# Ten tiles of the shared FFN computed in pieces among the experts of a sparse layer, added to the output in two groups

## The reference

```
scores = softmax(xf @ gate_w.T)                     # 64 experts
topk_w, topk_idx = top_k(scores, 6)
buf_tok[e], buf_w[e] = the rows of expert e and their weights   # 128 slots an expert
gx = xf[buf_tok]                                    # gather, (64, 128, 512)
g, u = split(gx @ gate_up_proj)                     # 64 x (512, 384)
eo = (silu(g) * u) @ down_proj * buf_w              # 64 x (192, 512)
routed = zeros.at[buf_tok].add(eo)                  # scatter with addition
shared = (silu(xf @ shared_gate.T) * (xf @ shared_up.T)) @ shared_down.T   # inner size 384
x = x + routed + shared
```

## Time and profile before

| | |
|---|---|
| median of three runs | 1262.53 us |
| the profiled execution | 1266.02 us |
| its span, first to last instruction | 1263.9 us |
| TensorE busy | 1150.1 us (91%) |
| VectorE, ScalarE, GpSimd busy | 829.8, 548.4, 697.2 us |
| DMA | 204.89 MB, mean 162 GB/s |
| first instruction of `c_up` / last one's start | 857.0 / 1241.0 us |

### The profile page before, as it was taken

The page is one execution under the profiler, slowest core; times in us unless marked ns, Lnnn a source line. Parts: engine busy times, 40 slices in busy tenths (PEclk is TensorE's granted clock), DMA queues, the critical chain, the costliest instruction groups (busy, mean ns, idle before and its releaser), DMA issues.

```text
span 1263.9 us, 17889 instructions
## 1 busy us (share of the span) xinstructions
PE 1150.1 (91%) x5241; PEld 877.6 (69%) x5241; DVE 829.8 (66%) x1369; ACT 548.4 (43%) x1012; POOL 697.2 (55%) x404
## 2 busy tenths in 40 slices
PE   2999999999999999999879999999888989888884
PEld 1777777777777777777768889986555656555552
DVE  1677787778777777877679994645555555545543
ACT  5455555555556555654412222214334443334331
POOL 4988988888898889887030000012433544444342
PEclk8999999999999999999889999999999899889987
DMA  6224423432343244332376344456999999999995
GB/s 198 75 74 121 118 81 102 120 102 81 118 120 100 81 120 120 90 100 69 123 169 198 101 124 121 114 156 179 304 287 287 260 308 293 271 287 277 305 244 86
DMA packets 93402, 204.89 MB, mean 162 GB/s; under 512 B 15495, under 2 KB 24455, under 8 KB 93232
## 3 DMA queue, kind: packets, MB, share of 16 engines
q1 hardware_dynamic: 78256, 168.23, 45.0%
q0 software_dynamic: 15104, 36.16, 12.5%
HBM read 152.65 MB, written 52.22 MB: 162 GB/s over the span
## 4 chain that ended last, share of the span: by engine, by line
PE 57%; DMA 19%; issue 8%; DVE 8%; ACT 4%; POOL 2%; SPq 1%; POOLq 0%; DVEq 0%; ACTq 0%
PE Y L546 10%; PE Y L421 8%; PE Y L423 7%; PE Y L422 7%; DMA out_dram<-o,idx_b 6%; DMA out_dram<-w,idx_b 5%; PE Y L630 4%; DMA stage<-xn_rows,idx_i 4%; PE Y L425 3%; PE OT L564 3%; PE DX L564 3%; PE DX L404 2%; ACT xn L758 2%; PE DX L444 2%; DVE s L1147 2%
## 5 line engine op out<-in xcount | busy, mean ns | idle before, releaser
L970 POOL TENSOR_TENSOR ring<-vT,cT 128x1024 f32<-128x1024 f32 x128 | 249.2, 1957 | 73.5 <-ACT vT L738 38.7
L421 PE MATMUL Y<-split,toep 128*128 128x512 f32 x576 | 250.4, 435 | 10.2 <-POOL split L978 10.2
L1102 DVE TENSOR_TENSOR z<-Y,cT 128x1024 f32<-128x1024 f32 x128 | 156.1, 1220 | 125.1 <-PE Y L425 89.4
L978 POOL TENSOR_TENSOR split<-ring,split 128x1024 fp32r<-128x1024 f32 x96 | 230.0, 2396 | 0.0
L423 PE MATMUL Y<-split,toep 128*128 128x512 f32 x576 | 228.5, 397 | 0.0
L422 PE MATMUL Y<-split,toep 128*128 128x512 f32 x576 | 228.3, 396 | 0.0
L630 PE MATMUL Y<-ring,xT 128*128 128x384 f32 x512 | 203.4, 523 | 14.6 <-DMA ring<-in_L_ffn_down_proj_dram 14.6
L1014 POOL DMA_INDIRECT stage<-xn_rows,idx_i x64 | 68.8, 1075 | 222.7 <-issue 207.4
L546 PE MATMUL Y<-split 128*128 128x384 f32 x768 | 152.0, 347 | 4.2 <-DVE split L1161 4.2
L1107 DVE TENSOR_REDUCE o<-z 128x128 f32<-128x1024 f32 x128 | 154.4, 1206 | 1.1
L546 PEld LDWEIGHTS Y<-split 128*128 128x128 f32 x768 | 137.9, 194 | 7.5 <-DVE split L1161 3.0
(11 more groups left out here) (150 smaller groups left out, 1872.9 us busy)
## 6 DMA issues: line engine op xcount, KB each, us to landing
ring<-_L_ffn_gate_up_proj_dram SPq DMA_DIRECT2D x64, 768.0 KB
ring<-in_L_ffn_down_proj_dram SPq DMA_DIRECT2D x64, 384.0 KB
gr<-filters SPq DMA_DIRECT2D x32, 512.0 KB, 3.8
stage<-in_x_dram SPq DMA_DIRECT2D x32, 256.0 KB, 3.5
stage<-in_ctx_dram SPq DMA_DIRECT2D x32, 256.0 KB, 3.7
x_rows<-stage SPq DMA_DIRECT2D x32, 256.0 KB, 3.2
xn_rows<-xn SPq DMA_DIRECT2D x32, 256.0 KB, 3.3
xT_rows<-xT SPq DMA_DIRECT2D x32, 256.0 KB, 2.8
```

What stands on the lines that cost most here:

```text
L421: pe.matmul(y, high, kv[:, s, 0, a, n], start=(a == 0), stop=False)
L970: pool.tensor_tensor(to.rearrange("p (b j i) -> p b j i", i=NH, j=NH), a, d, ALU.mult).then_inc(kvp_ready, 1)
L978: pool.tensor_tensor(kv[:, s, 1, c, :], kvp[c], kv[:, s, 0, c, :].bitcast(F32), ALU.subtract).then_inc(kv_ready, 1)
L1102: dve.tensor_tensor(zz[c % 2].rearrange("p (b j i) -> p b j i", j=NH, i=NH), YY[c % 2][:, :].rearrange("p (b j i) -> p b j i", j=NH, i=NH) ...
```

## The change

NB = 22 tiles stay in the shared FFN's pipeline. Tile 22 is computed in one go at its end, by new functions `late_*` that use one set of buffers and the PSUM banks Y[2] and Y[3]. The tiles 23 to 31 are computed among the experts: each odd expert up to 53 gets one of the pieces gate, up, out (`pieces`), three odd experts for a tile. Their results are copied to six buffers in SBUF (`y2`). GpSimd adds them to the output by accumulating DMAs in two groups of five tiles, after the scatters of the pairs 12 and 27 (`batches`, `add_shared`). The residual of these ten tiles is stored straight to the output in the convolution stage (`late=True`). The 16 steps over [64, 256] now stand behind the tiles 19, 20 and 21, six, six and four of them, and the lists are turned at tile 22. The broadcast of a list row is a matmul with a one-hot matrix into a free part of bank Y[0], in place of the DMA. The experts' results rotate through two PSUM banks in place of four, and some buffers move to other memory.

```diff
+        def pieces(e):
+
+            n = (e - 1) // 2
+            t = NB + 1 + n // 3
+            return (t, "gate up out".split()[n % 3]) if e % 2 and t < NT else (None, None)
+
+        def batches(k):
+
+            return [n for n in range((NT - NB) // BATCH) if k == 3 * ((n + 1) * BATCH - 1)]
...
-            def store(h, s):
+            def store(h, s, late):
                 sp.wait_ge(x1_ready, h + 1)
-                sp.dma_start(rows(x1_rows, h), x1[:, s, :]).then_inc(x1_out[s], 16)
+                sp.dma_start(rows(out[0:T, :] if late else x1_rows, h), x1[:, s, :]).then_inc(x1_out[s], 16)
...
-            b_iteration(MOVE_AT, 0)
-            b_iteration(MOVE_AT + 1, 1)
             sp.wait_ge(first_ready, NF)
             sp.dma_start(both[:, CAP:], firsts[E:2 * E, :]).then_inc(half_in, 16)
-            with sp.Fori(MOVE_AT // 2 + 1, NT // 2 - 1) as i:
-                b_iteration(i * 2, 0)
-                b_iteration(i * 2 + 1, 1)
-            def load_row(n):
-                if n >= 2:
-                    sp.wait_ge(same_ready, n - 1)
-                row = chosen_rows[2 * n]
-                sp.dma_start(rowa[:, n % 2, :], bass.AP(row.tensor, row.offset, [[0, P], [1, CAP]])).then_inc(row_in[n % 2], 16)
-
-            b_iteration(NT - 2, 0, fetch_xT=False)
-            sp.wait_ge(chosen_ready, NF)
-            sp.dma_start(chosen_rows, chosen).then_inc(chosen_out, 16)
-            b_iteration(NT - 1, 1, fetch_xT=False, fetch_x1=False)
-            sp.wait_ge(chosen_out, 16)
-            for n in range(2):
-                load_row(n)
-            b_store(NT - 1, 1)
-
+            for t in range(MOVE_AT, NB):
+                b_iteration(t, t % 2, fetch_x1=(t + 1 < NB))
+            b_store(NB - 1, 1)
+            b_load_xT(NB + 2, 0)
 
             for e in range(E):
-                if e % 2 and e // 2 + 2 < E // 2:
-                    load_row(e // 2 + 2)
+                t, part = pieces(e)
+                if part == "up" and t + 2 < NT:
+                    b_load_xT(t + 2, t % 2)
                 if e + NW < E:
                     sp.wait_ge(c_down, e + 1)
                     weights(sp, e + NW, e % NW)
...
-            with pe.Fori(0, 13) as i:
+            with pe.Fori(0, NB // 2 - 2) as i:
                 b_iteration(i * 2 + 3, 1)
                 b_iteration(i * 2 + 4, 0)
-            for t in range(NT - 3, NT):
-                b_iteration(t, t % 2)
-            b_turn_hid(NT - 1, 1)
-            pe.wait_ge(y_ready, NT - 2)
-            b_out(NT - 1, 1)
+            b_iteration(NB - 1, 1)
+
+            def late_half(t, g):
+                pe.wait_ge(b_xT_lo, t + 1)
+                if t == NB:
+                    pe.wait_ge(b_hid, NB)
+                elif g:
+                    pe.wait_ge(y2_ready, t - NB)
+                else:
+                    pe.wait_ge(b_hT_lo, t)
+                for c in range(NC):
+                    for a, b in ((0, 0), (0, 1), (1, 0)):
+                        last = pe.matmul(Y[2 + g][:, 0:SI], xTs[:, t % 2, a, c, :], sh_gu[:, b, c, g * SI:(g + 1) * SI],
+                                         start=(c + a + b == 0), stop=(c == NC - 1 and a == 1))
+                last.then_inc(up_ps if g else gate_ps, 1)
+
+            def late_turn_hid(t):
+                pe.wait_ge(b_hid, t + 1)
+                for a in range(n_up):
+                    last = pe.transpose(Y[2][:, a * P:(a + 1) * P], hid2[:, a * P:(a + 1) * P], ident)
+                last.then_inc(b_hT_ps, 1)
+
+            def late_out(t):
+                pe.wait_ge(b_hT_lo, t + 1)
+                for c in range(n_up):
+                    for a, b in ((0, 0), (0, 1), (1, 0)):
+                        last = pe.matmul(Y[3][:, :], hTs2[:, a, c, :], sh_d[:, b, c, :],
+                                         start=(c + a + b == 0), stop=(c == n_up - 1 and a == 1))
+                last.then_inc(b_down, 1)
+
+            b_turn_hid(NB - 1, 1)
+            late_half(NB, 0)
+            turn_chosen()
+            pe.wait_ge(y_ready, NB - 2)
+            b_out(NB - 1, 1)
+            late_half(NB, 1)
+            late_turn_hid(NB)
...
             def c_up(e, part):
                 s, r = e % 2, e % NW
+                if s == 0 and part == 0:
+                    if e:
+                        pe.wait_ge(same_ready, e // 2)
+                    pe.matmul(Y[0][:, SI:SI + CAP], ident[0:E, e:e + 1].to_broadcast([E, P]), chosen, start=True, stop=True)
...
-                if e >= 4:
-                    pe.wait_ge(eb_ready if s else ea_ready, e // 2 - 1)
+                if e >= 2:
+                    pe.wait_ge(eb_ready if s else ea_ready, e // 2)
                 for c in range(2):
                     for a, b in ((0, 0), (0, 1), (1, 0)):
-                        last = pe.matmul(c_dn[e % 4][:, :], hTs[0:IH, s, a, c, :], c_d[:, s, b, c, :],
+                        last = pe.matmul(DN[s][:, :], hTs[0:IH, s, a, c, :], c_d[s][:, b, c, :],
...
             def c_iteration(e):
                 pe.wait_ge(c_xT_sb, e + 1)
+                t, part = pieces(e)
                 if e + 1 < E:
                     c_turn(e + 1)
+                if part == "out":
+                    late_turn_hid(t)
                 pe.wait_ge(weights_in[e % NW], (e // NW) * 32 + 32)
                 if e >= 2:
                     pe.wait_ge(c_hid, e - 1)
@@ -672,12 +714,18 @@
                 c_up(e, 1)
                 if e % 2 and e > 1:
                     c_move(e // 2 - 1)
+                if part == "gate":
+                    late_half(t, 0)
+                if part == "up":
+                    late_half(t, 1)
+                if part == "out":
+                    late_out(t)
                 if e:
                     c_out(e - 1)
...
+            def late_gate(t):
+                act.wait_ge(gate_ps, t + 1)
+                act.wait_ge(b_hid, t)
+                act.activation(sg2, Y[2][:, 0:SI], ACT.Silu).then_inc(b_silu, 1)
+
+            def late_evacuate_hid(t):
+                act.wait_ge(b_hT_ps, t + 1)
+                act.wait_ge(b_down, t)
+                act.activation(hTs2[:, 0, :, :].rearrange("p c n -> p (c n)"), Y[2][:, 0:SI], ACT.Copy).then_inc(b_hT_sb, 1)
+
+            def late_result(t):
+                n = t - NB
+                act.wait_ge(b_down, t + 1)
+                if n == 0:
+                    act.wait_ge(prob_out, B * 16)
+                    act.wait_ge(y_ready, NB)
+                elif n >= NY2:
+                    act.wait_ge(y2_added, (n - NY2) // BATCH * BATCH * 16 + BATCH * 16)
+                act.activation(y2[n % NY2], Y[3][:, :], ACT.Copy).then_inc(y2_ready, 1)
+
+            b_evacuate_hid(NB - 1, 1)
+            late_gate(NB)
+            b_evacuate(NB + 1, 1)
+            late_evacuate_hid(NB)
+            late_result(NB)
...
+                t, part = pieces(e)
                 if e + 1 < E:
                     c_evacuate(e + 1)
+                if part == "out":
+                    late_evacuate_hid(t)
                 if e:
                     c_evacuate_hid(e - 1)
                 c_gate(e)
                 c_down_high(e)
+                if part == "gate":
+                    late_gate(t)
+                if part == "up" and t + 1 < NT:
+                    b_evacuate(t + 1, (t + 1) % 2)
+                if part == "out":
+                    late_result(t)
...
+            def add_shared(n, k):
+                for a in range(2):
+                    pool.wait_ge(added[a], (k + 1) * 16)
+                for t in range(NB + n * BATCH, NB + (n + 1) * BATCH):
+                    pool.wait_ge(y2_ready, t - NB + 1)
+                    pool.dma_start(rows(out[0:T, :], t), y2[(t - NB) % NY2], accum_op=ALU.add).then_inc(y2_added, 16)
+                pool.wait_ge(y2_added, (n + 1) * BATCH * 16)
+
             for s in range(2):
-                pool.wait_ge(y_out[s], NT // 2 * 16)
+                pool.wait_ge(y_out[s], NB // 2 * 16)
+                pool.wait_ge(x1_out[s], NT // 2 * 16)
             for k in range(E // 2):
                 for e in range(2 * k + NG - 2, min(2 * k + NG, E)):
                     fetch(e)
                 for a in range(2):
                     add(k, a)
+                for n in batches(k):
+                    add_shared(n, k)
...
             b_iteration(MOVE_AT, 0)
-            b_iteration(MOVE_AT + 1, 1)
-            for t in range(MOVE_AT + 2, NT):
+            for t in range(MOVE_AT + 1, NB):
                 b_iteration(t, t % 2)
-                for n in range((t - MOVE_AT - 2) * 2, (t - MOVE_AT - 2) * 2 + 2):
-                    if n < NF:
-                        chosen_best(n)
+                first = (t - MOVE_AT - 1) * 6
+                for n in range(first, min(first + 6, NF)):
+                    chosen_best(n)
                     if n < NF - 1:
                         chosen_out(n)
-            b_hidden_low(NT - 1, 1)
-            b_result(NT - 1, 1)
+
+            def late_hidden(t):
```

(26 more changed lines are left out.)

81 lines of the change are left out of this document (42 added, 39 removed).

## The result

| | median | runs | profiled execution | span |
|---|---|---|---|---|
| before | 1263.79 us | 4 | 1266.02 us | 1263.9 us |
| after | 1280.59 us | 4 (1277.04 to 1282.66) | 1277.04 us | 1275.2 us |

The ratio of after to before is 1.0125, 95% interval 1.0083 to 1.0168. The forecast was 1258.4 us, 4 faster. All ratios in this text leave out four executions that took over 1.5% more than the fastest of their kernel, one of which (with the row by DMA) took 1659 us.

What follows compares the result with a forecast made beforehand. TensorE was taken to bound the shared FFN, DMA and GpSimd's scatter chain the experts. Terms -41.0 + 14.9 + 10.5 + 11.5 = -4.1 us gave 1258.4 from the median; likeliest case 1250 to 1270, 8 in 10 1238 to 1283.

Steps and rivals of the forecast that it cites:

- The shared FFN and its seam: Shared FFN to first expert: nine tiles leave -59.4, list-step bursts +12.4, seam at tile 22 +6, together -41.0 us.
- The change of bound: Among the experts: a pair of 12.66 us on TensorE exceeds the scatters' 12.29, so the stops vanish.
- The piece itself: Among the experts: a third of a tile for each of 27 odd experts adds 2.20 us to a pair's 10.26.
- The bank rotation: Experts' results, two banks for four: copy wait hidden under the 2.1 us piece; may cost 0.5 in five pairs without one.
- The stall at the first group: First group of additions, before expert 32: its gather, queued behind the group, comes late; +10.5 us, ends 3 and 20.
- a third of one of 384 ... so 0.2: Broadcast matmul of 128 columns in each pair of experts, priced at 0.2 us from a row showing two in 1.46.
- TensorE's standstill ends the demand for weights: Groups of additions: argument against long groups, that a stopped TensorE asks for no more weights; five accumulations taken at 10.1 us.
- long groups: Rival (0.25): groups share engines with weights, five accumulations take 18 to 20 us, stalls 19 and 18; +17, 1279 us.
- The sum by that rule, +16: Whole kernel, if engines go round-robin between queues: groups get half, each stall some 10 us longer, sum +16.
- the links behind the second group: From pair 27's scatter: next scatter at 25.5, three links of 9, last one 11.4, end at 64 us; term +11.5.
- Short groups: Rival (0.30): five accumulations overlap, 1.31 MB in 4.5 us, stalls of 4 and 5; -17, 1245 us.
- pieces free: Rival (0.05): pairs of experts stay at 12.11 us and groups are short; -32, 1231 us.

## Why the prediction was wrong

**What held.** The shared FFN and its seam (-41.0; measured -42.6, with a spread of 10 us between executions), with the stops, the blocks of list steps and the loss of clock where they were put. The change of bound (TensorE without a gap, scatters behind it, no stops between). The piece itself: 10.26 + 2.20 is the period of the kernel with the row by DMA. The bank rotation, whose copy lies under the piece. In a pair without a piece I had 0.5 for the copy; it is 12.02 - 10.26 - 0.64 = 1.1, in the pairs from expert 54 on.

**What came out right by luck.** The stall at the first group, 10.22 us where I had 10. The gather went out 1018.47 - 991.89 = 26.6 us after the scatter of pair 12, 4 later than my 22.5; TensorE had its rows 1022.34 - 1018.47 = 3.9 us after that, where I had allowed 7.5. The two errors cancel. And the pair lost 12.5 us, not 10.5: behind the stall the clock is at half, which I had priced at 1.7 us behind each block of list steps and at nothing here, without a reason. (That 1.7 was itself read from two views: 3.82 is from start to end, 2.08 from start to start; in one view it is 3.82 - 2.24 = 1.6.)

**What failed, first: "a third of one of 384 ... so 0.2".** The broadcast was priced by its columns, and rounded down at that: a third of half of 1.46 is 0.24. It takes 0.5 in the row and 0.64 a pair, so the pair came to 13.0 instead of 12.66, and 27 x 0.39 = 10.5 us were missing. The term measured 7.9 over, since the first pair has no result of a predecessor in it and takes only 10.33. In the kernel before, the same 0.64 costs nothing. It was dear because the change itself had made TensorE the bound. My own sum had said so ("this is above the scatters' 12.29"), which was the reason to price every new instruction on TensorE to the tenth of a microsecond from a row of its own kind. There was none before, and I took the far row at its lower value without a bound from above.

**Second: "TensorE's standstill ends the demand for weights".** It does, but too late. The first group began at 1003.48 us and TensorE stood still from 1012.1; the weights issued at 1006.90 and 1012.15 were on their way, and only then came none until 1032.43. So 2.31 MB of weights went beside the first group's 1.31 MB. The engine time of an accumulation (8.8 us for five) was rather below my 2.0 each, and the groups still lasted 15.0 and 17.1 where I had 12.5. The likeliest reason is that they did not have the engines for themselves: the two queues' shares add up to 102.6% during the first. But during the second, from 1211 to 1227 us, they are 50.9% and 41.5%, so there the engines had a little left; and no run tested a group without weights beside it. It is the mechanism of the rival "long groups", at 15 to 17 us instead of its 18 to 20, and past the 14 from which I had said that it decides. The Trainium skill (DMA: Bandwidth & Descriptors, "SWDGE vs HWDGE vs iDMA") says that the engines go round-robin between GpSimd's queue and the others. The shares of 58.9% and 43.7% during the first group agree with it in that both queues were served side by side, GpSimd's with the larger share. The sum by that rule, +16, was nearer to the 11.3 of the spans and the 17 of the medians than mine, but not in each term: it puts the first stall at 20.5, which came to 12.5, and the end at 21.5, which came to 18.6, and the 7.9 of the broadcast, which it doesn't have, fill most of the gap. I had written the rule down and then gone by a row of the tail, where only one queue had work.

**Third: the links behind the second group.** I let the next scatter leave 25.5 us after the one of pair 27. It left after 1230.44 - 1199.20 = 31.2: the group began at 11.5 instead of 10 and lasted 17.1 instead of 12.5; the two gathers behind it took 2.7, near the 3 forecast. Three links took 31.1 instead of 27, and from the last scatter to the end 13.7 instead of 11.4, with the clock at half behind the stall. Together that is 76.0 us from the scatter of pair 27 to the end, 12 more than the 64 forecast and the largest single miss; 4.6 of it is the second point again. But this scatter left 22.4 us behind the start of expert 54, before 29.8, which is 7.4 us less where I had credited 2.5, and so the ledger shows 7.1 of the 12.

**Of the rivals:** "long groups" (0.25, 1279 us) is what came, by its mechanism; that its number nearly came too is in part luck. Its 6 us of stops between the pairs were not there, the 7.9 of the broadcast stood in their place, and its first stall of 19 came to 12.5. "Short groups" and "pieces free" are excluded by the 15.0 us and by 13.0 a pair.

**What is left open:** why a lone small matmul stands for 0.4 to 0.5 us when a second one adds 0.22; how much of a group's length the weights beside it make; why the chain of scatters is slower with the row by DMA; and the 5 us between the median and the trace of the kernel with the list steps alone.
